# In each pipeline step, TensorE issues the scores for the row maxima ahead of the scores for the exponential

## The reference

```python
x = x + retention(layernorm(x))     # rotary q, k; (q k^T) * decay mask * v; group norm; Wo
x = x + block2(layernorm(x))

def block2(x):
    h = rms(x, n1_w)
    q, k, v = rms(heads(wq), qn_w), rms(heads(wk), kn_w), heads(wv)
    scores = einsum('bhqd,bhkd->bhqk', q, k) * 8 ** -0.5     # causal
    attn = softmax(scores, axis=-1)
    x = x + (attn @ v) @ wo.T            # first 32 channels of the update are zero
    xf = rms(x, n2_w)
    # router: softmax over 4 experts, the top 2 renormalised; all 4 experts are computed
    return x + sum_e wts_e * expert_e(xf)
```

## Time and profile before

| what | value |
|---|---|
| median of 3 runs | 1119.94 us (1115.63 to 1126.91) |
| profiled execution, its own time | 1120.34 us |
| its span in the trace | 1118.6 us |
| mean granted TensorE clock | 0.777 of 2.4 GHz |
| TensorE busy | 930.4 us |
| ACT, DVE, POOL busy | 526.7, 512.7, 369.7 us |

### The profile page before, as it was taken

The page is one execution under the profiler, slowest core; times in us unless marked ns, Lnnn a source line. Parts: engine busy times, 40 slices in busy tenths (PEclk is TensorE's granted clock), DMA queues, the critical chain, the costliest instruction groups (busy, mean ns, idle before and its releaser), DMA issues.

```text
span 1118.6 us, 16258 instructions
## 1 busy us (share of the span) xinstructions
PE 930.4 (83%) x6192; PEld 553.9 (50%) x6192; DVE 512.7 (46%) x1123; ACT 526.7 (47%) x1072; POOL 369.7 (33%) x595
## 2 busy tenths in 40 slices
PE   2655778899889989898989888998899889889767
PEld 1534634654545546463646454564546444444534
DVE  2334366445643664446653564365635642434021
ACT  1315215534644546454745464464746445434524
POOL 5324224314521534234622542153513421311311
PEclk9667656756878876896899887887989679758759
DMA  4000000000000000000000000000000000000000
GB/s 146 1 10 1 1 10 1 1 1 11 1 1 2 21 1 2 1 2 20 2 1 1 20 2 0 2 11 1 1 1 11 1 1 1 11 1 1 11 0 10
DMA packets 13724, 9.04 MB, mean 8 GB/s; under 512 B 2128, under 2 KB 13136, under 8 KB 13648
## 3 DMA queue, kind: packets, MB, share of 16 engines
q1 hardware_dynamic: 13648, 8.00, 2.4%
HBM read 5.64 MB, written 2.10 MB: 7 GB/s over the span
## 4 chain that ended last, share of the span: by engine, by line
PE 69%; DVE 17%; ACT 8%; issue 4%; POOL 2%; DMA 1%; SPq 0%; POOLq 0%; ACTq 0%; DVEq 0%
PE side L464 14%; PE outs L400 10%; PE side L349 7%; PE scores L380 7%; DVE mneg L872 6%; PE side L452 5%; PE maxima L362 5%; PE side L500 5%; PE side L421 4%; PE maxima L365 4%; PE outs L440 4%; ACT p L649 4%; PE side L447 3%; DVE p L882 2%; DVE hB L1009 2%
## 5 line engine op out<-in xcount | busy, mean ns | idle before, releaser
L872 DVE TENSOR_REDUCE mneg<-maxima 128x2 f32<-128x256 f32 (+3 forms) x256 | 211.1, 824 | 333.4 <-PE maxima L365 332.1
L1094 POOL TENSOR_SCALAR_AFFINE_SELECT p<-p 128x256 f32<-128x256 f32 x256 | 107.6, 423 | 416.7 <-ACT p L649 416.4
L649 ACT ACTIVATE p<-scores 128x1024 f32<-128x1024 f32 (+3 forms) x256 | 180.2, 704 | 127.7 <-PE scores L380 126.7
L380 PE MATMUL scores<-qs,ks 25*128 25x256 f32 (+3 forms) x512 | 125.9, 488 | 39.9 <-ACT p L649 39.1
L362 PE MATMUL maxima<-ks,qs 24*128 24x384 f32 (+3 forms) x512 | 110.2, 427 | 35.9 <-DVE mneg L872 35.0
L400 PE MATMUL outs<-p,v2x 128*32 128x512 f32 (+3 forms) x1024 | 117.6, 594 | 1.0 <-POOL p L1094 1.0
L380 PEld LDWEIGHTS scores<-qs,ks 25*128 25x128 f32 x512 | 56.6, 217 | 110.3 <-ACT p L649 59.0
L1102 POOL TENSOR_SCALAR_AFFINE_SELECT p<-p 128x512 f32<-128x512 f32 x64 | 40.7, 636 | 155.9 <-ACT p L658 155.9
L362 PEld LDWEIGHTS maxima<-ks,qs 24*128 24x128 f32 x512 | 59.2, 228 | 60.2 <-DVE mneg L872 56.5
L882 DVE TENSOR_TENSOR p<-side,sb_t_tri 128x512 f32<-128x512 f32 x64 | 44.1, 690 | 92.3 <-PE side L421 92.3
L421 PE MATMUL side<-qs,ks 24*128 24x128 f32 x512 | 52.6, 331 | 38.7 <-DVE p L882 36.6
(11 more groups left out here) (154 smaller groups left out, 1508.7 us busy)
## 6 DMA issues: line engine op xcount, KB each, us to landing
x_in<-x_dram SPq DMA_DIRECT2D x8, 256.0 KB, 2.9
qs<-mT SPq DMA_DIRECT2D x128, 2.0 KB
out_dram<-yout SPq DMA_DIRECT2D x8, 256.0 KB, 2.3
sb_t_cos<-t_cos_dram SPq DMA_DIRECT2D x1, 512.0 KB, 4.9
sb_t_sin<-t_sin_dram SPq DMA_DIRECT2D x1, 512.0 KB, 4.9
sb_w_l<-w_l_dram SPq DMA_DIRECT2D x2, 256.0 KB
sb_w_qkv<-w_qkv_dram SPq DMA_DIRECT2D x2, 192.0 KB, 3.6
sb_w_u<-w_u_dram SPq DMA_DIRECT2D x3, 128.0 KB
```

The costliest lines, as they stand in the source:

```text
L380: last = nc.tensor.matmul(eb[:, i, 0:n], ks[rows, b % 2, g, 128 * kt:128 * kt + 128], qs[rows, b % 2, g, 128 * kt:T], start=True, stop=True)
L649: A_(p2[kt][:, 2 * hp:2 * hp + 2, :], eb[:, :, 0:n], ACT.Exp, scale=float(D) ** -0.5).then_inc(exp_done, 1)
L872: V.tensor_reduce(mneg[:, g, 2 * hp:2 * hp + 2, qt], mb[:, :, 0:128 * (qt + 1)], AX.X, ALU.max, negate=True)\
L1094: Q.affine_select(out=diag, in_=diag, compare_op=ALU.is_ge, fill=0.0, base=0, pattern=[[0, 2], [1, 128]], channel_multiplier=-1).then_inc( ...
```

## The change

The two calls change places in TensorE's program. Nothing else changes: not the other engines' programs, not the waits, not the buffers.

```diff
                 for s in range(G * GK):
-                    exponents(it, s)
                     if on(it):
                         maxima(it, s)
+                    exponents(it, s)
                     if s in WEIGH_AT:
                         off, g, half = WEIGH_AT[s]
                         weigh(it + off, g, half)
```

## The result

The changed kernel takes 1178.64 us (median of 5 runs, 1177.88 to 1185.41), the kernel before 1119.07 beside it (1115.63 to 1126.91): a ratio of 1.0527 [1.0482, 1.0573]. The forecast was 1144 with a range up to 1164, so the direction was right, the size less than half of what came, and the result lies outside the range. The profiled execution took 1185.41 us (span 1183.7) at a mean granted clock of 0.761, where it was 0.777 before: 65 us more on the same basis.

The account below looks back on a forecast made before the run. TensorE, busy 83% of the span, was taken to bound the kernel. Terms 1.5 + 0.3 + 1.0 + 0.3 + 0.1 = 3.2 us per iteration, together 24 us on 1120.3, gave 1144 us, range 1123 to 1164.

Parts of the forecast that it names:

- the rival for the clock: Added pauses lower the granted clock by 0.10 in six iterations: another 18 us, 1162 in all; chance 0.13.
- the term for the joints: Streaming steps pay 0.18 us more with full-size filling first, 0.09 with `weigh` first: 1.5 us per iteration, bounds 0 and 3.5.
- M to N: Start of maxima matmuls to start of mask matmuls: in both orders, 0.28 us for 384 columns, so no added cost.
- N to E: Start of mask matmuls to start of exponent matmuls: 0.21 us in the changed trace.
- E to F: Start of exponent matmuls to start of filling: 0.25 to 0.43 us by width, 0.09 dearer than exponents to maxima.
- Short bare runs: Steps 3 to 4, 8 to 9 and 10 to 12, without filling: 0.3 us in all, bounds 0 and 0.8.
- Steps 15 to 20: Width jump puts unit 16's exponential behind DVE's reduction, then step 20's filling comes later: 1.0 us, bounds 0.3 and 1.8.
- Steps 25 to 31: Steps 25 to 28, where ACT is late: +0.3 us, bounds -0.5 and +0.8; steps 29 to 31: 0.1.
- the rival for a faster kernel: Maxima and mask matmuls slip into waits for late ACT in steps 4, 9, 12, 27, 28: -11 us, 1109; chance 0.06.
- 0.3 to 7.5 an iteration: The prediction's own case at its bounds, in us, called further than believed; with terms mixed about 1128 to 1162.
- step 5 up to `weigh` 0.80: Sign at full clock, in the step the prediction called 13: 0.80 us up to `weigh`, where it took 0.71.
- the waits of E for ACT: Sign: TensorE's exponent matmuls wait for ACT about as long as before, when it was 39.1 us.

Follow-up runs that it names:

- joint: Kernel before, with one eight-column bf16 matmul with full-size weights put between exponent and maxima matmuls in every step; 1186.72 us, 1.0596 of before.
- mask_last: Against the kernel before: maxima matmuls first, exponents straight behind them, mask matmuls last, in all steps; 1142.95 us against 1132.08.
- combo: Kernel before with the edits of `joint_bare` and `before_warm_more` together; 1135.62 us, 1.0083 of before.
- after_delay: Changed kernel with 32 bf16 matmuls added once, ahead of step 0 of iteration 1; 1186.17 us, 1.0573 of before.
- first_0_7: Kernel before with maxima ahead of exponents in steps 0 to 7 only; 1134.80 us against 1132.08.
- first_21_31: Kernel before with maxima ahead of exponents in steps 21 to 31 only; 1134.78 us against 1132.08.
- mask_last_2: The edit of `mask_last` measured again; 1145.44 us against 1126.07 for the kernel before.
- after_warm_more: Changed kernel with six zero-weight matmuls ahead of each of steps 3, 4, 8, 10, 11, 12, 15 and 16; 1170.18 us, 1.0425 of before.
- joint_bare: Kernel before with the eight-column matmul of `joint` only in the nine steps without filling; 1110.38 us, 0.9893, and again 1114.41, 0.9889.
- before_warm: Kernel before with six zero-weight matmuls of 128 columns ahead of each of steps 8, 10, 11, 15 and 16; 1117.08 us, 0.9856.
- before_warm_more: The edit of `before_warm` on the kernel before, with six zero-weight matmuls also ahead of steps 3, 4 and 12; 1109.71 us, 0.9893.

## Why the prediction was wrong, step by step

Two steps of it failed. The larger: the sum put the clock at nothing, and the rival for the clock priced it at 18 us from the means of two iterations, where steps 4 and 5 and the places alone lose 6.2 us an iteration to it. The smaller: the term for the joints (1.5) took M to N to be the same in both orders, where it is 0.10 us dearer after the change; by the steps that can be read the term is about 2.6.

**The joints: right in kind, too small.** The prediction took 0.18 us for a step with full-size filling and found 0.28 to 0.29. N to E is 633.52 - 633.31 = 0.21 as read from the earlier trace rows, and E to F with 512 columns is 0.43, within the 0.25 to 0.43 named. What failed is the line "M to N is in both orders". It is, but it isn't equally long: with 128, 256, 384 and 512 columns it takes 0.16, 0.21, 0.27 and 0.38 us before and 0.26, 0.31, 0.37 and 0.43 after (medians at full clock). Before, M followed E, matmuls of the same shape; now it opens its own run, behind full-height work. The rest of the 0.29 is as predicted. `joint` shows the same 0.10 with nothing reordered.

The Trainium skill, "TensorEngine Tiling (Array Packing)", Key Properties, says that each change of the mode drains TensorE. The prediction set this aside for M to N because the earlier trace rows had it cheap. The runs side more with the page: a change into 24-row work and one out of it together cost 0.29 us where a run was split. They don't follow it in all, though: M to N is a change of mode in both orders and yet has two prices. Whether it is a drain, or a weight load that no longer hides, no run here separates. In streaming steps (0, 1, 14, 22, 23) it was +0.28 to +0.34 each and in those with `weigh` first (5 at full clock, 21) +0.2, where 0.09 was forecast. The term of 1.5 comes to about 7 x 0.29 + 3 x 0.2 = 2.6 by these; steps 6 (+0.13) and 24 (+0.57) don't fit the one price.

**Short bare runs:** 0.3 predicted, 0.45 in steps 7 to 12. Right within what can be read.

**Steps 15 to 20: right.** The kernel after, iteration 4, against the earlier trace rows:

```profile
675.69 0.29 PE L365 MATMUL maxima<-negb,idb 128*128 128x128 bf16 x2
...
677.30 0.32 PE L362 MATMUL maxima<-ks,qs 24*128 24x128 f32 x2 [1.06 <-DVE mneg L872]
...
677.77 0.50 PE L380 MATMUL scores<-qs,ks 25*128 25x512 f32 x2
...
679.39 0.79 PE L380 MATMUL scores<-qs,ks 25*128 25x512 f32 x2 [0.23 <-ACT p L649]
680.11 1.51 PE L400 MATMUL outs<-p,v2x 128*32 128x256 f32 x16
...
686.88 0.69 PE L362 MATMUL maxima<-ks,qs 24*128 24x384 f32 x2 [1.73 <-DVE mneg L872]
...
688.33 1.97 PE L349 MATMUL side<-sb_t_id,oT 128*128 128x128 f32 x8
```

Counted from the mask matmuls of step 15: M of step 16 at 1.61 us (1.60 forecast), E of step 16 at 2.08 (2.15), E of step 17 at 3.70 (3.76), `weigh` at 4.42 (4.3). From M of step 20 to the filling 1.45 (1.4). The step lengths show the give-back too: +1.65 in step 19 and -1.68 in step 20. In sum +1.45 where 1.0 was taken, inside the bounds of 0.3 and 1.8. The exponential of unit 16 now stands behind the reduction and not beside it: this is what the change of order itself costs, and `mask_last` agrees with its +1.0 and +1.7%.

**Steps 25 to 31:** +0.3 and +0.1 predicted; steps 25 to 30 gave -1.4 in sum. ACT's lateness did let M N slip in, as the rival for a faster kernel had it: at full clock step 26 is 0.80 shorter, 25 and 27 are 0.15 and 0.18 shorter, against +0.57 in step 24, at whose end M of step 25 waits for DVE. Step 28 (+0.88) and step 29 (-0.97) are mostly clock, which varies there in the kernel before. The forecast's sign was wrong; steps 25 to 28 together changed by -0.25, less than the 0.5 named as a sign.

**The bounds.** "0.3 to 7.5 an iteration" isn't the sum of the bounds given: these come to about -0.1 and 7.0. Even 7.0 in every iteration would give 1172, short of the 1178.6 measured: within their bounds these terms alone don't reach the result.

**Outside the clock** the 9.5 us an iteration are 3.3 when the 6.2 are taken off, and 4.4 by length times clock, where the prediction had 3.2. With the factor used there (6 whole iterations and 4.6 / 3.2 = 1.4 for the two others) 4.4 is 33 us or 1153: inside the range. That the sum comes so near is in part luck: the joints were too small and steps 25 to 31 too large.

**The clock: a rival that came true, at the wrong place and the wrong price.** It had 0.13 and 18 us. It was to act through a fall of 0.10 in an iteration's mean, at 3 us per 0.10, a price worked out from two iterations with different work in them. Neither holds. The mean fell by only 0.016, and what would have shown the prediction wrong, a shift by over 0.03, didn't occur. But two executions of the kernel before on one chip (beside `combo`) had clocks of 0.762 and 0.783 and spans of 1130.9 and 1115.4 us: 15.5 us for 0.021. And what counts isn't the mean but where the low stretch stands. In steps 4 and 5 TensorE has work without a pause, and there it now falls; that is 3.9 us an iteration, and another 2.3 in the places. Together 6.2 of the 9.5 us. Counted in other ways the share is smaller. Span times clock is 869 us before and 900 after: 31 us more at full clock. They would take 40 us at the old mean clock (31 / 0.777), which leaves 25 of the 65 us to the clock; taken at full clock they leave 34. Between four tenths and two thirds of the loss is what I would claim.

The chain is then: the split runs and the wait behind the reduction lengthen the iteration by 3.3 to 4.4 us, and more of its busy steps fall into stretches at the lower clock. The first link is shown, by `joint` (the split alone, the same time and mean clock) and `mask_last` (no split, a quarter to two fifths of the loss). That the lower clock takes the rest is shown by the rows at either level. Why it falls where it does is not: `after_delay`, the fixed lengths and steps 4 and 5 of `first_0_7`, which run at either level with one and the same program, speak for its depending on when the work comes, and the pattern of steps 4 and 5 isn't needed for the loss, since `joint` loses as much with another. By what rule the clock chooses was not tried and stays open, as does whether the parts of the change add up and why `combo` loses.

**The signs named in advance:** N to E 0.21, right; E to F by width, right; step 5 up to `weigh` 0.80, wrong: its counterpart in iteration 4 runs at the lower clock and takes 1.45 (648.21 - 646.76), but step 21, with the same widths at full clock, takes 0.90, and so does step 5 of `first_0_7` in iterations 2 to 5, so that M to N's 0.10 is missing here too; steps 15 to 17 and 20, right; the waits of E for ACT "about as long as before", wrong (39.1 to 16.5 us); iterations 1 to 5 at 129.7 to 132.8 us and so above 126, as forecast (iteration 6 has less work than the prediction gave it: 99.4 us before, 106.8 after).

## What to carry to other kernels

Before putting a small matmul between two of another weight shape, count the runs of equal shape that are split, not only the joints whose neighbours change: a run's first matmul is dearer than the same matmul inside it. In a periodic loop whose clock changes within each turn, price a change by where the low-clock stretches would fall, step by step, and not by the mean clock; a few us more in an iteration can cost twice as much in the end, and a matmul in a true wait can gain. The two gains that were combined here didn't add, so try such edits one place at a time and repeat them: of six ways to put filler matmuls into the kernel before, three gained 1.1 to 1.4%, and the other three, the combination of two winners among them, lost 0.8 to 6%.

## What the runs showed that I had not expected

- **Iterations settle at fixed lengths.** 129.70 us (three in a row within 0.01) in all three profiles of the changed kernel and with an added delay; 119.44 with nine tiny matmuls, twice. Others settle too: `first_21_31` at 122.7 to 122.9, the last two iterations of `mask_last_2`, `after_warm_more` and `combo` at 126.3. `joint` goes to and fro between 127.8 and 135.1.
- **Added matmuls in waits made the kernel faster.** Five groups of six zero matmuls raised the mean granted clock to 0.799 and took 1.4% off; nine eight-column ones raised it to 0.79 to 0.80 and took 1.1% off, twice. `joint_bare`, `before_warm` and `before_warm_more` all beat both kernels of this case; the lowest time is that of `before_warm_more`, 1109.71 us.
- **The clock works in stretches that a step can be in or out of.** The same `weigh` of step 5 takes 1.71 us at a granted clock of 1.00 and 3.08 in a stretch at 0.57, in two kernels that differ in an order of matmuls.
- **A fixed length without a cause in the program.** The Trainium skill, "TensorE: Matmul & The Clock Gate", Part 1, says that the gate judges activity in windows that run on by themselves and don't start with the kernel. The iterations that come back to one length after a delay, and steps 4 and 5 of `first_0_7`, which run at either level, agree with a judgement that depends on when work comes; that they settle on a length is not on the page, and no run here shows the windows themselves.
